# Attention scores on two 64-row tiles of TensorE, both halves of a token tile issued together

## Chip, cores and metric

One core of one Trainium2 chip. The metric is the device time of one execution, in microseconds (us). Lower is better.

## What is computed

Two batches of 1024 tokens of width 256 go through cross-attention to 64 context rows (16 heads of width 16) and then through a mixture of 8 experts, of which each token takes 2. Cut to what matters here:

```
q = layernorm(x) @ w_q.T + b_q;  k = ctx @ w_k.T + b_k;  v = ctx @ w_v.T + b_v      # heads of 16
scores = einsum('bhqd,bhkd->bhqk', q, k) / sqrt(16) + log(key_abundance)
x = x + softmax(scores) @ v @ w_o.T + b_o
x = x + experts(layernorm(x))     # softmax gate, top 2 of 8, silu(x w1) * (x w3) @ w2
```

Everything is float32. The kernel splits the operands of the larger products into two float16 parts (high and low) and adds three products: high by high, high by low, low by high.

## The kernel before

The work has three stages. A preparation (to about 45 us) loads and transposes the weights, makes keys and values, and splits them. The attention stage (to about 180 us) takes the 16 tiles of 128 tokens one per step, with tile `tt` of batch `tt % 2`. The expert stage (from about 210 us) takes 39 tiles of 128 routed tokens. All engines run a program written out by hand (`attention_steps`), with one semaphore for each product; each engine works through its own instructions strictly in order.

**The keys for the scores.** A head has only 16 rows of the contraction. To use all 128 rows of TensorE, `spread_keys` (L799 to L805, on VectorE) writes the keys of 8 heads into a block matrix `kb_hi`, `kb_lo` of 128 rows by 8 x 64 = 512 columns: `head_mask` keeps, for each head, its own 16 rows and clears the other 112. There are four such products for each batch (two groups `c` of 8 heads, high and low), at L803.

**The scores.** `scores_half(par, c)` (L1164 to L1172) makes the scores of 8 heads for 128 tokens in one PSUM bank of `sc_ps`: three matmuls of 512 columns with the query tile (L1169 to L1171) and one of 512 columns that adds the bias and the logarithm of the abundance (`beta`, L1172). One call for `c` = 0 stands at the start of a step, the other for `c` = 1 in its middle.

**One step on TensorE**, in order of the program: scores `c` = 0 of tile t (L1169 to L1172); the product of probabilities and values of tile t-2 (L1204, 8 float32 matmuls, 16 passes); the transpose of the normalized tokens of tile t+1 (L1149); the transpose for the second layer norm of tile t-4 (L1220); scores `c` = 1 of tile t; the transpose of the attention output of tile t-2 (L1232), which waits for `o_norm` and for `xt_lo`; the queries of tile t+1 (L1160 to L1162, 12 matmuls of 128 columns); the transposes of the probabilities of tile t-1 (L1247); the gate's logits of tile t-4 (L1260); the output projection of tile t-2 (L1271, L1272).

**What VectorE and ScalarE do in the same step.** VectorE: maximum of the first 8 heads (L898), reciprocal of the softmax sums (L917, waits for L1204), the scaling of the output (L929, gives `o_norm`), the low part of the next tokens (L834, waits for ScalarE's L632 and gives `xt_lo`), maximum of the other 8 heads (L898 again), subtraction (L945), the low part of the queries (L828), logits (L957), residual (L965), statistics (L970, L906). ScalarE: exponential (L659), high part of the tokens (L632, waits for L1149), two layer norms (L624, L677), L684, the high float16 part of one piece of expert weights (L587), L694, L639, and two copies of the transposed probabilities (L701).

**The expert weights** are prepared beside all this: SyncE loads a piece, ScalarE makes its high part (L587) and GpSimd its low part (L488). Steps 4, 5, 14 and 15 take two pieces, the others one. GpSimd also makes the scale of the second layer norm (L506, L510, L513), behind the pieces that were issued before it.

The product with the values takes the heads pairwise: transposed block `j` holds the probabilities of the two heads that lie at columns 128 j of `sc_ps`, and `v_blk` has the values of heads 2 j and 2 j + 1 in block `j`.

Of the kernel before, what the change touches and what calls it, by code (L numbers as in the profile page):

```python
# [5 lines left out]
ALU = mybir.AluOpType  # L6
ACT = mybir.ActivationFunctionType
F32 = mybir.dt.float32
F16 = mybir.dt.float16
# [3 lines left out]
P = 128  # L13
# [4 lines left out]
def xattn_moe(nc, x, ctx_in, abundance, w_in, b_in, w_out, b_out, gate_w, expert_bias, w1, w2, w3, out):  # L18
# [7 lines left out]
    B, N, D = x.shape  # L26
    S2 = ctx_in.shape[1]
    HD = 16
    H = D // HD
    E, _, F = w1.shape  # L30
# [7 lines left out]
    HS = SL // 2  # L38
    TOPK = 2
    J = (TOK * TOPK + E * (P - 1)) // P  # L40
    NOUT = HD + 1
# [8 lines left out]
    with ExitStack() as stack:  # L50
# [33 lines left out]
        take = Region(arena)  # L84
        xs = take(T * D).rearrange("p (t d) -> p t d", t=T)

        kb_hi, kb_lo = (take(2 * B * HS, F16).rearrange("p (c b n) -> p c b n", c=2, b=B) for _ in range(2))

        wq_hi, wq_lo = (take(KD * D, F16).rearrange("p (k n) -> p k n", k=KD) for _ in range(2))
        xT_hi, xT_lo = take(KD * P, F16), take(KD * P, F16)  # L90
        qT_hi, qT_lo = ([take(2 * P, F16) for _ in range(2)] for _ in range(2))
# [96 lines left out]
        bias16 = take(B * H, F16)  # L188
        ones_row = take(P)[0:1]
        head_mask = take(8)  # L190
        zero_rows = take(D)

        FIRST = 4
# [97 lines left out]
        def here(t, lag):  # L291

            return t is None or 0 <= t - lag < T
# [277 lines left out]
        def _(act):  # L571
# [62 lines left out]
            def queries_high(tt, par):  # L634

                act.wait_ge(s["q_ps"], tt + 1)
                if not isinstance(tt, int) or tt >= 2:
                    act.wait_ge(s["s_ps"], 2 * (tt - 1))
                act.activation(qT_hi[par], bk7[:, 0:2 * P], ACT.Copy).then_inc(s["q_hi_s"], 1)  # L639

            act.wait_ge(s["ln1_shift"], 1)
# [104 lines left out]
        def _(dve):  # L746
# [13 lines left out]
            for c in range(2):  # L760
                dve.tensor_scalar(bq_blk[:, c, :], head_mask[:, :], bias_qk[:, c:c + 1], None, ALU.mult)\
                    .then_inc(s["bq_s"], 1)

            dve.wait_ge(s["ctxT_ps"], 1)
            for k in range(KD):
# [33 lines left out]
            def spread_keys(b):  # L799

                for c in range(2):
                    for dst, src in ((kb_hi, kT_hi), (kb_lo, kT_lo)):
                        dve.tensor_tensor(dst[:, c, b, :].rearrange("p (h s) -> p h s", h=8),  # L803
                                          src[:, c, b:b + 1, :].broadcast_to([P, 8, S2]),
                                          head_mask[:, :, None].broadcast_to([P, 8, S2]), ALU.mult).then_inc(s["kb_dve"], 1)  # L805

            spread_keys(0)

# [80 lines left out]
            def step(u, par, t):  # L889
# [3 lines left out]

                def maxima(c):

                    dve.wait_ge(s["s_ps"], 2 * tt + c + 1)
                    hh = slice(c * H // 2, (c + 1) * H // 2)
                    dve.tensor_reduce(top[:, hh], sv[:, hh, :], AX.X, ALU.max).then_inc(s["smax"], 1)  # L898

# [186 lines left out]
        def _(pe):  # L1086
# [49 lines left out]
            pe.wait_ge(s["bq_s"], 2)  # L1136
            for b in range(B):
                for c in range(2):
                    ins = pe.matmul(bk6[:, b * H + c * 8:b * H + (c + 1) * 8], kT[:, c, b].rearrange("p r s -> p (r s)"),
                                    bq_blk[:, c, :], start=True, stop=True)  # L1140
            ins.then_inc(s["bias_ps"], 1)

            def x_transpose(tt, par):
# [18 lines left out]
                        ins = pe.matmul(o, wq_lo[:, k, cc], xT_hi[:, kk], start=False, stop=k == KD - 1)  # L1162
                ins.then_inc(s["q_ps"], 1)

            def scores_half(par, c):

                o = sc_ps[par][:, c * HS:(c + 1) * HS]
                cc = slice(c * P, (c + 1) * P)
                pe.matmul(o, qT_hi[par][:, cc], kb_hi[:, c, par, :], start=True, stop=False)  # L1169
                pe.matmul(o, qT_hi[par][:, cc], kb_lo[:, c, par, :], start=False, stop=False)  # L1170
                pe.matmul(o, qT_lo[par][:, cc], kb_hi[:, c, par, :], start=False, stop=False)  # L1171
                return pe.matmul(o, ones16[:, :], beta[:, par, c * HS:(c + 1) * HS], start=False, stop=True)  # L1172

            pe.wait_ge(s["bias_parts"], 1)
            x_transpose(0, 0)
# [4 lines left out]
            def step(u, par, t):  # L1180
                tt = 2 * u + par
                if here(t, 0):
                    pe.wait_ge(s["q_lo_s"], tt + 1)
                    if t is None or t >= 2:
                        pe.wait_ge(s["ssub"], tt - 1)
                    elif t == 0:
                        pe.wait_ge(s["kb_dve"], 4)
                        pe.wait_ge(s["beta_s"], 1)
                    elif t == 1:
                        pe.wait_ge(s["kb_dve"], 8)  # L1190
                        pe.wait_ge(s["beta_s"], 2)
                    scores_half(par, 0).then_inc(s["s_ps"], 1)
                if here(t, 2):

                    bt = tt - 2
                    pe.wait_ge(s["pt_sb"], 2 * (bt + 1))
                    if t is None or bt >= 1:
                        pe.wait_ge(s["o_norm"], bt)
                    else:
                        pe.wait_ge(s["v_sb"], 4 * B)  # L1200
                    if here(t, 0):
                        pe.wait_ge(s["q_lo_s"], tt + 1)
                    for j in range(8):
                        ins = pe.matmul(bk7[:, j * 2 * NOUT:(j + 1) * 2 * NOUT], probT[par][:, j * P:(j + 1) * P],  # L1204
                                        v_blk[:, par, j, :], start=True, stop=True)
                    ins.then_inc(s["o_ps"], 1)
                if here(t, -1):
                    if t is None or t >= 3:
# [4 lines left out]
                if here(t, 4):  # L1213
# [5 lines left out]
                    for k in range(KD):  # L1219
                        ins = pe.transpose(pt_ps2[:, k * P:(k + 1) * P], xn2[par][:, k * P:(k + 1) * P], idt)  # L1220
                    ins.then_inc(s["x2t_ps"], 1)
                if here(t, 0):
                    scores_half(par, 1).then_inc(s["s_ps"], 1)
                if here(t, 2):
                    bt = tt - 2
                    pe.wait_ge(s["o_norm"], bt + 1)
# [166 lines left out]
```

## Time and profile before

| | |
|---|---|
| median of 3 runs | 497.25 us (494.78 to 498.67) |
| the profiled execution | 492.84 us |
| its span in the profile | 491.1 us |
| TensorE busy | 402.9 us, 82% of the span |
| VectorE, ScalarE, GpSimd busy | 272.4, 194.7, 223.9 us |
| chain of work that ended last | TensorE 72%, VectorE 11% |

The times of rows are those of the profiled execution, counted from the start of its span; the 1.74 us between its span and its time lie around the program. A row of the timeline has the start, the duration and the engine, then line, operation, what is written and read, and in brackets how long the engine sat idle before it and what ended that. A matmul's recorded duration holds its latency; what it costs in a stream is the distance from its start to the start of the next.

### The profile page before, as it was taken

The numbers are of one execution on the slowest core, as the hardware profiler recorded it, in microseconds if no ns is written. First come the engines' busy times: TensorE is split into PE (matmuls) and PEld (weight loads), VectorE is DVE, ScalarE is ACT, GpSimd is POOL, SyncE is SP. The second block draws the span as 40 slices with busy tenths as digits, with TensorE's granted clock in tenths as the row PEclk, the third lists the DMA queues.
The fourth block names the chain that finished last, engine by engine and source line by source line (L and its number), as shares of the span: only waits on it lengthen the run. The fifth ranks groups of instructions, "written<-read, shape, count | busy, mean of one in ns | idle before, by whom it ended". The sixth has DMA issues, their size and how long they took to land.

```text
span 491.1 us, 10557 instructions
## 1 busy us (share of the span) xinstructions
PE 402.9 (82%) x2969; PEld 303.1 (62%) x2970; DVE 272.4 (55%) x635; ACT 194.7 (40%) x351; POOL 223.9 (46%) x277
## 2 busy tenths in 40 slices
PE   4526998999997531159999999999999999999960
PEld 4303877787776421027777777777777777777740
DVE  2697766767664178915555455555555554555530
ACT  2525677577575433013233323333333333333310
POOL 3694455444446457023444444444444444444321
PEclk9667999999998755569999999999999999999985
DMA  8621442324263623011222222222222222222215
GB/s 263 209 91 61 157 140 86 114 102 133 75 194 108 207 68 92 1 33 24 39 39 43 43 43 43 32 43 35 42 43 43 43 41 35 42 35 43 34 21 182
DMA packets 29267, 38.35 MB, mean 78 GB/s; under 512 B 5173, under 2 KB 23874, under 8 KB 29218
## 3 DMA queue, kind: packets, MB, share of 16 engines
q1 hardware_dynamic: 21440, 27.60, 17.7%
q0 software_dynamic: 7488, 10.39, 13.5%
q8 instruction: 9, 0.15, 0.1%
q10 hardware_dynamic: 322, 0.15, 0.1%
q14 instruction: 8, 0.07, 0.0%
HBM read 28.62 MB, written 11.60 MB: 82 GB/s over the span
## 4 chain that ended last, share of the span: by engine, by line
PE 72%; DVE 11%; issue 4%; DMA 4%; POOL 3%; ACT 3%; POOLq 0%; SPq 0%; DVEq 0%; ACTq 0%
PE sc L1337 10%; PE sc L1339 10%; PE sc L1338 10%; PE ptps L1327 6%; PE bank L1360 6%; PE bank L1356 5%; PE bank L1358 4%; PE bank L1204 4%; PE bank L1271 3%; PE ptps L1247 3%; DVE arena L803 2%; PE bank L1309 2%; DMA arena<-in_x 2%; PE bank L1260 1%; DMA stage_w<-in_L_ffn_w 1%
## 5 line engine op out<-in xcount | busy, mean ns | idle before, releaser
L563 POOL DMA_INDIRECT acc<-arena,put_now x39 | 62.5, 1603 | 113.9 <-DVE arena L1075 113.9
L1337 PE MATMUL sc<-w_hi,arena 128*128 x312 | 98.3, 315 | 1.0 <-DVE arena L1053 1.0
L1338 PE MATMUL sc<-w_hi,arena 128*128 x312 | 98.3, 315 | 0.0
L1339 PE MATMUL sc<-w_lo,arena 128*128 x312 | 98.3, 315 | 0.0
L488 POOL TENSOR_TENSOR w_lo<-stage_w,w_hi 128x1408 f16<-128x1408 f32 (+3 forms) x32 | 73.6, 2312 | 43.7 <-ACT w_hi L587 43.7
L1065 DVE SCALAR_TENSOR_TENSOR arena<-sc,slot_score,arena 128x352 f32<-128x352 f32 (+1 forms) x117 | 53.0, 480 | 66.2 <-ACT arena L734 66.2
L734 ACT ACTIVATE arena<-sc,slot_score 128x352 f32<-128x352 f32 x78 | 43.3, 555 | 89.7 <-PE sc L1339 89.7
L1356 PE MATMUL bank<-w_hi,arena 128*128 x234 | 64.4, 275 | 2.2 <-DVE arena L1080 2.2
L1360 PE MATMUL bank<-w_lo,arena 128*128 x234 | 64.8, 277 | 0.0
L741 ACT ACTIVATE arena<-ptps 128x768 f16<-128x768 f32 x39 | 31.7, 812 | 83.4 <-PE ptps L1327 83.4
L1078 DVE TENSOR_TENSOR arena<-ptps,arena 128x640 f16<-128x640 f32 x39 | 32.2, 825 | 44.4 <-ACT arena L741 44.4
L538 POOL DMA_INDIRECT arena<-table,get_now x39 | 39.7, 1017 | 33.2 <-POOL get_now L535 32.1
L1358 PE MATMUL bank<-w_hi,arena 128*128 x195 | 53.7, 276 | 0.0
L1339 PEld LDWEIGHTS sc<-w_lo,arena 128*128 128x128 f16 x312 | 30.7, 99 | 16.4
L1337 PEld LDWEIGHTS sc<-w_hi,arena 128*128 128x128 f16 x312 | 30.7, 99 | 15.8 <-issue 1.4
L1338 PEld LDWEIGHTS sc<-w_hi,arena 128*128 128x128 f16 x312 | 30.8, 99 | 14.8
L535 POOL COPY get_now<-arena 128x1 int32 (+1 forms) x39 | 28.0, 718 | 22.0 <-DVE arena L1029 15.3
L587 ACT ACTIVATE w_hi<-stage_w 128x1408 f16<-128x1408 f32 (+3 forms) x32 | 35.0, 1104 | 7.3 <-DMA stage_w<-in_L_ffn_w 7.3
L1327 PE MATMUL ptps<-ident,arena 128*128 128x128 f32 x234 | 34.1, 282 | 1.2 <-DVE arena L1065 1.2
L1204 PEld LDWEIGHTS bank<-v_blk,w_lo 128*128 128x128 f32 x256 | 30.9, 192 | 2.2
L1204 PE MATMUL bank<-v_blk,w_lo 128*128 128x34 f32 x256 | 29.9, 272 | 0.0
L1360 PEld LDWEIGHTS bank<-w_lo,arena 128*128 128x128 f16 x234 | 22.9, 98 | 10.8 <-issue 8.4
(198 smaller groups left out, 708.4 us busy)
## 6 DMA issues: line engine op xcount, KB each, us to landing
stage_w<-in_L_ffn_w SPq DMA_DIRECT2D x16, 704.0 KB, 4.3
stage_w<-in_L_ffn_w SPq DMA_DIRECT2D x16, 256.0 KB, 2.8
arena<-in_x SPq DMA_DIRECT2D x2, 1024.0 KB, 7.1
stage_w<-in_L_ffn_w SPq DMA_DIRECT2D x32, 64.0 KB, 2.7
acc<-arena SPq DMA_DIRECT2D x16, 128.0 KB, 1.7
table<-xn SPq DMA_DIRECT2D x16, 128.0 KB, 1.8
arena<-table,get_now POOLq DMA_INDIRECT x39, 2.8
acc<-arena,put_now POOLq DMA_INDIRECT x39, 3.8
```

The source lines that it names most:

```text
L488: pool.tensor_tensor(w_lo[:, cols], staged[:, :], w_hi[:, cols], ALU.subtract).then_inc(s["wlo"], 1)
L563: pool.indirect_dma_start(out=acc[:, :], out_offset=bass.IndirectOffsetOnAxis(ap=put_now[q][:, 0:1], axis=0), in_=y_sb[q], in_offset=None, ...
L734: act.activation(sil[par].rearrange("p (c n) -> p c n", c=2)[:, c, :], h1_ps[:, c, :], ACT.Silu, scale=slot_score[par][:, 0:1]).then_inc(s ...
L1065: dve.scalar_tensor_tensor(out=hid[par][:, at:at + b - a], in0=h3_ps[:, c, a - c * FH:b - c * FH], scalar=slot_score[par][:, 0:1], in1=sil ...
L1204: ins = pe.matmul(bk7[:, j * 2 * NOUT:(j + 1) * 2 * NOUT], probT[par][:, j * P:(j + 1) * P], v_blk[:, par, j, :], start=True, stop=True)
L1327: ins = pe.transpose(hT_ps[:, c * P:(c + 1) * P], hid[q][:, c * P:(c + 1) * P], idt)
L1337: pe.matmul(ps[:, c, :], gT_hi[par][:, kk], w_hi[:, cols], start=k == 0, stop=False)
L1338: pe.matmul(ps[:, c, :], gT_lo[par][:, kk], w_hi[:, cols], start=False, stop=False)
L1339: ins = pe.matmul(ps[:, c, :], gT_hi[par][:, kk], w_lo[:, cols], start=False, stop=k == KD - 1)
L1356: pe.matmul(bk7[:, 0:D], hT_hi[q][:, cc], w_hi[:, cols], start=c == 0, stop=False)
L1358: pe.matmul(bk7[:, 0:D], hT_lo[q][:, cc], w_hi[:, cols], start=False, stop=False)
L1360: ins = pe.matmul(bk7[:, 0:D], hT_hi[q][0:rows, cc], w_lo[0:rows, cols], start=False, stop=c == KF - 1)
```

## The change

`spread_keys` no longer clears all but 16 of 128 rows. It keeps a block of 4 heads for each half of 64 rows: `half_mask` (the sum of the two halves of `head_mask`, one small operation on VectorE) has 4 columns, and `kb_hi`, `kb_lo` have 256 columns for each group `c` where they had 512. Rows 0 to 63 of these 256 columns hold heads 0 to 3 of the group, rows 64 to 127 heads 4 to 7.

The scores of a token tile are then made at one place, at the start of the step: first the two `beta` matmuls of 512 columns, which open both PSUM banks, and then 12 matmuls of 64 rows and 256 columns. They come in pairs: one on rows 0 to 63 that adds to the first bank, one on rows 64 to 127 that adds to the second. The scores of the middle of the step are gone, and `s_ps` counts one for a tile where it counted two; both maxima of VectorE wait for that one. The heads lie in another order in `sc_ps`, so the bias is written in that order, and the product with the values takes its blocks by `jv`.

```diff
+        HQ = HS // 2
+        kb_hi, kb_lo = (take(2 * B * HQ, F16).rearrange("p (c b n) -> p c b n", c=2, b=B) for _ in range(2))
...
+            link(dve.tensor_tensor(half_mask[:, :], head_mask[:, 0:4], head_mask[:, 4:8], ALU.add))
...
-                        dve.tensor_tensor(dst[:, c, b, :].rearrange("p (h s) -> p h s", h=8),
-                                          src[:, c, b:b + 1, :].broadcast_to([P, 8, S2]),
-                                          head_mask[:, :, None].broadcast_to([P, 8, S2]), ALU.mult).then_inc(s["kb_dve"], 1)
+                        dve.tensor_tensor(dst[:, c, b, :].rearrange("p (h s) -> p h s", h=4),
+                                          src[:, c, b:b + 1, :].broadcast_to([P, 4, S2]),
+                                          half_mask[:, :, None].broadcast_to([P, 4, S2]), ALU.mult).then_inc(s["kb_dve"], 1)
...
-                    dve.wait_ge(s["s_ps"], 2 * tt + c + 1)
+                    dve.wait_ge(s["s_ps"], tt + 1)
...
-            def scores_half(par, c):
-
-                o = sc_ps[par][:, c * HS:(c + 1) * HS]
-                cc = slice(c * P, (c + 1) * P)
-                pe.matmul(o, qT_hi[par][:, cc], kb_hi[:, c, par, :], start=True, stop=False)
-                pe.matmul(o, qT_hi[par][:, cc], kb_lo[:, c, par, :], start=False, stop=False)
-                pe.matmul(o, qT_lo[par][:, cc], kb_hi[:, c, par, :], start=False, stop=False)
-                return pe.matmul(o, ones16[:, :], beta[:, par, c * HS:(c + 1) * HS], start=False, stop=True)
+            def scores(par):
+
+                for c in range(2):
+                    pe.matmul(sc_ps[par][:, c * HS:(c + 1) * HS], ones16[:, :], beta[:, par, c * HS:(c + 1) * HS],
+                              start=True, stop=False, skip_group_check=True)
+                for c in range(2):
+                    for q, kb, last in ((qT_hi, kb_hi, False), (qT_hi, kb_lo, False), (qT_lo, kb_hi, True)):
+                        for g in range(2):
+                            rows = slice(g * P // 2, (g + 1) * P // 2)
+                            at = g * HS + c * HQ
+                            ins = pe.matmul(sc_ps[par][:, at:at + HQ], q[par][rows, c * P:(c + 1) * P],
+                                            kb[rows, c, par, :], start=False, stop=last, skip_group_check=True)
+                return ins
...
-                    scores_half(par, 0).then_inc(s["s_ps"], 1)
+                    scores(par).then_inc(s["s_ps"], 1)
...
+                        jv = j % 4 // 2 * 4 + j // 4 * 2 + j % 2
+                        ins = pe.matmul(bk7[:, jv * 2 * NOUT:(jv + 1) * 2 * NOUT], probT[par][:, j * P:(j + 1) * P],
+                                        v_blk[:, par, jv, :], start=True, stop=True)
...
-                if here(t, 0):
-                    scores_half(par, 1).then_inc(s["s_ps"], 1)
```

TensorE in step 4, from its start to the transpose of the attention output. Before:

```order
L1169 MATMUL sc<-arena 128x512
L1170 MATMUL sc<-arena 128x512
L1171 MATMUL sc<-arena 128x512
L1172 MATMUL sc<-beta,ones 128x512
L1204 MATMUL bank<-v_blk,w_lo 128x34 x8
L1149 MATMUL bank<-ident,xn 128x128 x2
L1220 MATMUL ptps<-ident,xn 128x128 x2
L1169 MATMUL sc<-arena 128x512
L1170 MATMUL sc<-arena 128x512
L1171 MATMUL sc<-arena 128x512
L1172 MATMUL sc<-beta,ones 128x512
L1232 MATMUL bank<-ident,o_sb 128x128 x2
```

The same stretch in the changed kernel, whose L1179 is the row-tile matmul, L1214 the values' product, L1153, L1230 and L1240 the three transposes:

```order
L1172 MATMUL sc<-beta,ones 128x512 x2
L1179 MATMUL sc<-arena 128x256 x12
L1214 MATMUL bank<-v_blk,w_lo 128x34 x8
L1153 MATMUL bank<-ident,xn 128x128 x2
L1230 MATMUL ptps<-ident,xn 128x128 x2
L1240 MATMUL bank<-ident,o_sb 128x128 x2
```

Four matmuls of 512 columns stood between the transposes L1220 and L1232; nothing stands there now, and 14 matmuls stand ahead of the values' product where there were 4.

VectorE in the preparation, from the keys of batch 0 to the first maximum, before:

```order
L803 TENSOR_TENSOR arena<-w_hi,w_lo 128x512 [waits kT16]
L803 TENSOR_TENSOR arena<-w_hi,w_lo 128x512 x3
L810 TENSOR_TENSOR arena<-sc,arena 128x512 [waits wq_hi_s]
...
L828 TENSOR_TENSOR arena<-bank,arena 128x256 [waits q_hi_s]
L803 TENSOR_TENSOR arena<-w_hi,w_lo 128x512 x4
L786 BN_STATS w_lo<-arena 128x6 x4
L898 TENSOR_REDUCE top<-sc 128x8 [waits s_ps]
```

The same in the changed kernel:

```order
L806 TENSOR_TENSOR arena<-w_hi,w_lo 128x256 [waits kT16]
L806 TENSOR_TENSOR arena<-w_hi,w_lo 128x256 x3
L813 TENSOR_TENSOR arena<-sc,arena 128x512 [waits wq_hi_s]
...
L831 TENSOR_TENSOR arena<-bank,arena 128x256 [waits q_hi_s]
L806 TENSOR_TENSOR arena<-w_hi,w_lo 128x256 x4
L789 BN_STATS w_lo<-arena 128x6 x4
L901 TENSOR_REDUCE top<-sc 128x8 [waits s_ps]
```

The order is unchanged there; eight operations have half the columns.

## Rows read from the trace of the kernel before

**Rows 1.** TensorE in steps 2 to 5 and 6 to 13: length, busy (instructions), granted clock, DMA share, GB/s
```profile
48.10:78.30 30.20, 28.24 (x224) 1.00 0.41 134
78.31:138.95 60.64, 59.08 (x475) 1.00 0.34 109
```

**Rows 2.** TensorE's timeline in step 11
```profile
116.55 0.38 PE L1169 MATMUL sc<-arena 128*128 128x512 f16 x1
...
117.42 1.87 PE L1204 MATMUL bank<-v_blk,w_lo 128*128 128x34 f32 x16
119.12 0.42 PE L1149 MATMUL bank<-ident,xn 128*128 128x128 f32 x2
...
120.24 0.38 PE L1172 MATMUL sc<-beta,ones 128*128 128x512 f16 x1
120.56 0.41 PE L1232 MATMUL bank<-ident,o_sb 128*128 128x128 f32 x2
...
123.80 0.38 PE L1169 MATMUL sc<-arena 128*128 128x512 f16 x1
```

**Rows 3.** ScalarE and VectorE in step 11
```profile
119.57 0.38 ACT L632 ACTIVATE arena<-bank 128x256 f16<-128x256 f32 x1 [2.42 <-PE bank L1149]
...
119.32 0.26 DVE L917 RECIPROCAL o_inv<-bank 128x16 f32<-128x16 f32 x1 [0.20 <-PE bank L1204]
119.61 0.42 DVE L929 TENSOR_TENSOR o_sb<-bank,o_inv 128x256 f32<-128x256 f32 x1
119.99 0.42 DVE L834 TENSOR_TENSOR arena<-bank,arena 128x256 f16<-128x256 f32 x1
```

**Rows 4.** TensorE in step 16, which has no scores
```profile
157.22 1.87 PE L1204 MATMUL bank<-v_blk,w_lo 128*128 128x34 f32 x16
...
159.90 0.44 PE L1232 MATMUL bank<-ident,o_sb 128*128 128x128 f32 x2 [0.56 <-DVE o_sb L929]
```

**Rows 5.** TensorE's timeline in the expert stage, around a matmul on 64 rows
```profile
240.66 0.27 PE L1360 MATMUL bank<-w_lo,arena 128*128 x1
240.77 0.27 PE L1356 MATMUL bank<-w_hi,arena 128*128 x1
240.98 0.28 PE L1360 MATMUL bank<-w_lo,arena 64*128 x1
241.19 0.87 PE L1327 MATMUL ptps<-ident,arena 128*128 128x128 f32 x6
```

**Rows 6.** GpSimd in step 4, and TensorE in steps 5 and 15
```profile
67.69 5.68 POOL L488 TENSOR_TENSOR w_lo<-stage_w,w_hi 128x1408 f16<-128x1408 f32 x2 [2.67 <-ACT w_hi L587]
...
75.86 1.07 PE L1247 MATMUL ptps<-ident,w_hi 128*128 128x128 f32 x8 [1.25 <-ACT xn2T L684]
...
153.24 1.90 PE L1247 MATMUL ptps<-ident,w_hi 128*128 128x128 f32 x8 [2.74 <-ACT xn2T L684]
```

**Rows 7.** VectorE's and GpSimd's timelines, read from two points each, so later counts are smaller
```profile
24.96 8.63 DVE L803 TENSOR_TENSOR arena<-w_hi,w_lo 128x512 f16<-128x512 f16 x3
28.22 5.37 DVE L803 TENSOR_TENSOR arena<-w_hi,w_lo 128x512 f16<-128x512 f16 x2
...
24.45 13.45 POOL L488 TENSOR_TENSOR w_lo<-stage_w,w_hi 128x1408 f16<-128x1408 f32 x5
27.71 10.19 POOL L488 TENSOR_TENSOR w_lo<-stage_w,w_hi 128x768 f16<-128x768 f32 x4
```

**Rows 8.** TensorE and VectorE in step 1, and TensorE's busy time and clock after it
```profile
39.58 0.61 PE L1169 MATMUL sc<-arena 128*128 128x512 f16 x1 [0.94 <-DVE arena L828]
40.84 0.63 PE L1172 MATMUL sc<-beta,ones 128*128 128x512 f16 x1
...
41.58 0.69 DVE L898 TENSOR_REDUCE top<-sc 128x8 f32<-128x512 f32 x1 [2.05 <-PE sc L1172]
...
42.00:44.00 2.00, 1.60 (x4) 0.50 0.01 4
44.00:46.00 2.00, 1.12 (x16) 0.98 0.00 0
```

More of the change, by code:

```diff
@@ L85, in xattn_moe @@
         xs = take(T * D).rearrange("p (t d) -> p t d", t=T)
-        kb_hi, kb_lo = (take(2 * B * HS, F16).rearrange("p (c b n) -> p c b n", c=2, b=B) for _ in range(2))
+        HQ = HS // 2
+        kb_hi, kb_lo = (take(2 * B * HQ, F16).rearrange("p (c b n) -> p c b n", c=2, b=B) for _ in range(2))
         wq_hi, wq_lo = (take(KD * D, F16).rearrange("p (k n) -> p k n", k=KD) for _ in range(2))
@@ L190, in xattn_moe @@
         head_mask = take(8)
+        half_mask = take(4)
         zero_rows = take(D)
@@ L637, in queries_high @@
                 if not isinstance(tt, int) or tt >= 2:
-                    act.wait_ge(s["s_ps"], 2 * (tt - 1))
+                    act.wait_ge(s["s_ps"], tt - 1)
                 act.activation(qT_hi[par], bk7[:, 0:2 * P], ACT.Copy).then_inc(s["q_hi_s"], 1)
@@ L1138, in _ @@
                 for c in range(2):
-                    ins = pe.matmul(bk6[:, b * H + c * 8:b * H + (c + 1) * 8], kT[:, c, b].rearrange("p r s -> p (r s)"),
-                                    bq_blk[:, c, :], start=True, stop=True)
+                    o = bk6[:, b * H:(b + 1) * H].rearrange("p (g c h) -> p c g h", g=2, c=2)[:, c]
+                    ins = pe.matmul(o, kT[:, c, b].rearrange("p r s -> p (r s)"),
+                                    bq_blk[:, c, :].rearrange("p (g h) -> p g h", g=2), start=True, stop=True)
             ins.then_inc(s["bias_ps"], 1)
@@ L1203, in step @@
                     for j in range(8):
-                        ins = pe.matmul(bk7[:, j * 2 * NOUT:(j + 1) * 2 * NOUT], probT[par][:, j * P:(j + 1) * P],
-                                        v_blk[:, par, j, :], start=True, stop=True)
+                        jv = j % 4 // 2 * 4 + j // 4 * 2 + j % 2
+                        ins = pe.matmul(bk7[:, jv * 2 * NOUT:(jv + 1) * 2 * NOUT], probT[par][:, j * P:(j + 1) * P],
+                                        v_blk[:, par, jv, :], start=True, stop=True)
                     ins.then_inc(s["o_ps"], 1)
```

## The prediction

> **What bounds the kernel now.** I read the page first: TensorE is busiest and carries most of the chain that ended last. Then I cut the attention stage by step. In steps 6 to 13 TensorE is busy 59.08 of 60.64 us at full clock, in steps 2 to 5 28.24 of 30.20 us [rows 1]. That looks like a stage that gets shorter by whatever is taken off TensorE. Busy time does not say so, though: an engine that fills a wait with work that could stand elsewhere is just as busy. So the next view is the timeline of one step, and beside it those of VectorE and ScalarE.
>
> In step 11 the values' product starts at 117.42, the token transpose at 119.12, the last matmul of the second half of the scores at 120.24, and the transpose of the attention output (L1232) at 120.56 [rows 2]. A 512-column matmul takes 0.216 us of the stream: (117.42 - 116.55) / 4, or 0.87 for four. So the second half of the scores is through at 120.46, and L1232 starts 0.10 later. What it waits for is on VectorE: the reciprocal starts at 119.32, just behind the values' product, the scaling at 119.61, the low part of the tokens (L834) at 119.99, ending 120.41; 0.15 later TensorE goes on [rows 3]. L834 also needs ScalarE's L632, 119.57 to 119.95. Both ways start at TensorE's values' product or the transpose right behind it, and neither passes through the scores. From the start of the values' product to L1232 it is 3.14 us, and that is the time of this chain, not of TensorE's work. The second half of the scores has lain inside it for nothing.
>
> Step 16 shows the same place without scores and without L834: 157.22 to 159.90, 2.68 us, of which TensorE idles 0.56 waiting for the scaling L929 [rows 4]. With L834 (0.42 us more) behind it, one gets 3.1 again.
>
> **The change, part by part.**
>
> *The middle of the step.* Four matmuls, 0.87 us, go from inside the 3.14 us. TensorE has 1.70 us of values' product and about 0.5 of transposes left there (the second half of the scores, 0.87 long and through at 120.46, began at 119.59, 0.47 behind L1149), so it will stand idle for about 3.14 - 2.17 = 0.97 us before L1232. Gain: nothing. VectorE's second maximum need not wait for scores any more, but nothing in the step waits for it: its results go into the next step.
>
> *The start of the step.* What stands there is outside the chain and pays in full. Before: 0.87 us. After: two bias matmuls, 2 x 0.216 = 0.43; six pairs of 256 columns; and the change from 128 rows to 64 and back. A 256-column matmul takes 0.11 us (240.66 to 240.77). The expert stage has one matmul on 64 rows in each tile: from the matmul ahead of it 0.21 us and from it to the next 0.21 us, where 0.11 is usual [rows 5]. So each change of the row size costs 0.10, two of them 0.20.
>
> Whether the two matmuls of a pair run beside each other no row of this case shows. If they do fully, a pair costs 0.109 and six 0.65; if not at all, twelve cost 1.31. The start of the step becomes 0.43 + 0.20 + 0.65 = 1.28 us, or 1.94; with the changes of size hidden too it could be 1.08. I take 1.28: each of the two has its own half of the rows and a bank of its own, so nothing that they use is shared but the issue. So +0.41 us for a step, with bounds of +0.21 and +1.07.
>
> On this the Trainium skill speaks twice. Its page TensorE: Matmul & The Clock Gate (Part 3, packing small matmuls) has matmuls on different row groups run together, with some 4 ns between their starts; by that a pair would be 0.113, an estimate, and the step dearer by 0.02. Its page TensorEngine Tiling (Array Packing) (Key Properties) says that changing the tiling mode drains TensorE; the trace agrees, with the 0.10 of each change in rows 5. By the first page alone the change reads as a gain of 0.64 us a step on TensorE, 1.73 to 1.09; it is the chain of rows 3 that speaks against it.
>
> *In how many steps.* Scores are in steps 0 to 15. Steps 2, 3, 4 and 6 to 13 have the pattern above: 11 steps. In step 5, GpSimd works off two pieces of weights, 67.69 to 73.37, before it makes the scale of a layer norm, and TensorE waits 1.25 us for the result at 75.86; that wait swallows the 0.41. In step 15 the like wait is 2.74 us, at 153.24 [rows 6], on a load that was issued behind the residual at the end of step 13, so steps 14 and 15 are hidden as well. 11 x 0.41 = +4.5 us (bounds: 2.3 and 11.8).
>
> *The preparation.* The eight operations of `spread_keys` halve. The first four lie beside GpSimd's and ScalarE's way to the first tokens. The other four are exposed: TensorE's queries of tile 1 come behind them. There the operations take 3.26 us and not their own time: GpSimd's pieces start at 24.45 and 27.71, VectorE's operations end at 24.96 and 28.22, each 0.51 behind the start of the next piece [rows 7]. Read as: each of VectorE's waits for the whole of GpSimd's, then runs in 0.51, and GpSimd waits for it in turn. Halved, only the 0.51 shrinks, to some 0.25: 4 x 0.26 = 1.05 us. Bounds: nothing, and half of what they take in all, 8.63 / 2 = 4.3 for the last three and 0.26 for the first, 4.6.
>
> The Trainium skill's page SBUF — State Buffer (two separate sides) calls the port pair of VectorE and GpSimd an exclusive lock that the loser waits for in full, also when a VectorE operation has two SBUF inputs; the trace agrees, with the 0.51 of rows 7.
>
> Of that 1.05, step 1 gives most back. It runs at half the clock: four score matmuls take 4 x 0.42 = 1.68 us from 39.58 on, and VectorE's maximum starts at 41.58, 0.32 behind their end [rows 8]. Now the maximum needs all scores: at half clock, with every term twice its price at full clock (an estimate), 2 x 0.42 + 6 x 0.21 + 2 x 0.20 = 2.50. From 39.58 - 1.05 = 38.53 that is 41.03, and the maximum starts at 41.35, 0.2 earlier than before. Net -0.2 us (without overlap of the pairs 1.26 more, +1.0). `half_mask` is one operation of 4 columns on VectorE (less than the 0.26 of L917 with 16) ahead of L786, which waits for the load of x, and costs nothing; the reordered bias and blocks change no size.
>
> *The sum.* +4.5 - 0.2 = +4.3 us. Against the profiled execution 492.84 becomes 497.1; that execution was 4.4 below the median of the runs shown. On the median: 497.25 + 4.3 = 501.6.
>
> **The rivals.**
>
> *A, forecast: the chain holds, pairs overlap.* 501.6; its own range is 499.4 (changes of size hidden: +2.3 - 0.2) to 503.5. Chance 0.50.
>
> *B, the pairs do not overlap.* 11 x 1.07 + 1.0 = +12.8: 510.1. For it: no row shows two matmuls at once, and the 0.10 at each change of size looks like weights that are not loaded ahead; if that also happens from tile to tile, TensorE gets near this. Against: same size of tile all through the twelve. Chance 0.22.
>
> *C, the clock rises a step later.* The granted clock is 0.50 until 44 and 0.98 behind it [rows 8], after TensorE's scores from 39.58 on and 1.60 us of work in the 2 us from 42. In the changed kernel the scores of tile 1 end near 41.1 and nothing follows until the queries of tile 2, so the rise may come only in step 2. Its start and values' product (1.28 + 1.71 = 3.0 us) at half clock would cost up to 3.0 more; I take 2.0: 503.6. Chance 0.13.
>
> *D, the other side: TensorE's work is the bound and the wait is not.* If the chain of rows 3 could move ahead, the step would lose 1.73 - 1.28 = 0.45: -5.0 - 0.2 = -5.2, 492.0. It needs L1232 to start less than 2.7 us behind the values' product, in place of 3.14. For it: TensorE busy at 97%, and only 0.1 to 0.2 us of idle before L1232. Against: the rows of VectorE and step 16. It decides once L1232 comes 0.41 earlier. Chance 0.08.
>
> *E, sharing in place of waiting.* If VectorE's slow operations are slow in proportion to their size, the preparation gains 4.6, of which step 1 gives 1.05 - 0.2 = 0.8 back: 4.5 - 3.8 = +0.7, 498.0. Against: the two ends 0.51 behind GpSimd's. Chance 0.07.
>
> **How the numbers follow.** 1% is 5.0 us, about what a measurement of this kernel can tell from no change: faster is below 492.3, slower above 502.2. Faster: most of D, 0.06. Within: two thirds of A, all of E, some of C and D, 0.48. Slower: the rest of A, most of C and all of B, 0.46. The range leaves out D and the tail of B: 497.2 to 510.5. The predicted time is A's.
>
> **What would show it.** Right: in steps 6 to 13 an idle of 0.9 to 1.0 us before L1240 (the old L1232), put down to VectorE's L834 or L929; 3.1 to 3.2 us from the values' product to it; 1.3 us from the first bias matmul to the values' product; starts of a pair a few ns apart and pairs 0.11 apart; TensorE's busy time in the stage down, and the stage longer by some 4 us; GpSimd's pieces at 24 to 35 us shorter by about 0.26 each. Wrong: less than 0.5 us of idle there (D), 0.11 from each row-tile matmul to the next (B), a clock of 0.5 behind 45 us (C), or `spread_keys` of batch 1 taking half its 10 us (E). If the steps with a double piece grow as well, the count of 11 was wrong.

## The result, and the profile after

The changed kernel takes 505.85 us (504.27 to 506.24, 4 runs) where the kernel before takes 496.01 us in the same comparison (4 runs): ratio 1.0228, 95% interval 1.0189 to 1.0267. It is slower by 9.8 us by the medians, by 11 us by the ratio. The ratios of this document leave out executions more than 1.5% above the fastest of the same kernel (among them three of e4's ten, one of e7's ten and six of e12's ten), while medians and ranges are of all. The forecast was slower by 4.3 us. The direction and the place were right; the forecast was less than half of what came.

The page of the changed kernel, its first two parts:

```profile
span 503.7 us, 10743 instructions
...
PE 410.0 (81%) x3065; PEld 312.2 (62%) x3066; DVE 269.8 (54%) x636; ACT 195.4 (39%) x351; POOL 222.2 (44%) x277
...
PEclk9756998989989555558999999999999999999985
```

TensorE is busy 410.0 us, 7 more than before, although the scores of a tile take 1.28 us of it where they took 1.73. The last line says why to look at the clock: in the attention stage, from the fifth digit on, eights stand among the nines. In the timeline of two steps (matmul rows of the queries left out; L1172 bias, L1179 row tiles, L1214 values' product, L1240 transpose of the attention output) one sees what was forecast:

```profile
115.03 0.59 PE L1172 MATMUL sc<-beta,ones 128*128 128x512 f16 x2
115.55 0.83 PE L1179 MATMUL sc<-arena 64*128 64x256 f16 x12
116.31 1.97 PE L1214 MATMUL bank<-v_blk,w_lo 128*128 128x34 f32 x16
118.12 0.41 PE L1153 MATMUL bank<-ident,xn 128*128 128x128 f32 x2
...
119.64 0.41 PE L1240 MATMUL bank<-ident,o_sb 128*128 128x128 f32 x2 [0.89 <-DVE arena L837]
...
123.42 0.59 PE L1172 MATMUL sc<-beta,ones 128*128 128x512 f16 x2
```

The start of the step is 1.28 us (115.03 to 116.31) for 0.87 before, and L1240 waits 0.89 us where [rows 2] left 0.10. From the values' product to it are 3.33 us. The step shown is an even one (10), and those were the longer ones before as well: the values' product of step 10 started at 109.52, and L1232 came 3.22 us later:

```profile
112.74 0.41 PE L1232 MATMUL bank<-ident,o_sb 128*128 128x128 f32 x2
```

In the odd steps it is 3.25 us for the 3.14 of [rows 2]. So the stretch grew by 0.11 us in both kinds of step. That the pairs run beside each other shows in the same timeline read from two later points:

```profile
115.67 0.71 PE L1179 MATMUL sc<-arena 64*128 64x256 f16 x10
...
115.78 0.60 PE L1179 MATMUL sc<-arena 64*128 64x256 f16 x8
```

Ten of the twelve are left at 115.67 and eight at 115.78: two matmuls start at once (to within the hundredth that the rows show), the next two 0.11 later. VectorE's and ScalarE's side of the same step, to be held against [rows 3]:

```profile
118.65 0.38 ACT L634 ACTIVATE arena<-bank 128x256 f16<-128x256 f32 x1 [3.48 <-PE bank L1153]
...
118.32 0.26 DVE L920 RECIPROCAL o_inv<-bank 128x16 f32<-128x16 f32 x1 [0.69 <-PE bank L1214]
118.62 0.42 DVE L932 TENSOR_TENSOR o_sb<-bank,o_inv 128x256 f32<-128x256 f32 x1
119.07 0.42 DVE L837 TENSOR_TENSOR arena<-bank,arena 128x256 f16<-128x256 f32 x1
```

The same chain. L837 starts 2.76 us behind the start of the values' product where L834 started 2.57 behind it in [rows 3]: 0.11 is the longer values' product, and 0.08 is the even step, in which L834 started 2.65 behind it before the change too (112.17 for 109.52). What was not forecast is one step earlier in the same timeline:

```profile
110.17 0.44 PE L1240 MATMUL bank<-ident,o_sb 128*128 128x128 f32 x2 [0.81 <-DVE arena L837]
111.68 1.91 PE L1255 MATMUL ptps<-ident,w_hi 128*128 128x128 f32 x8
```

The eight transposes of the probabilities take 1.91 us of record, 1.04 in the steps around. TensorE ran at the lower of its two clock levels there, a granted clock of 0.50, which is half speed, as its stretches say (length, busy, granted clock, DMA share, GB/s):

```profile
76.50:79.50 3.00, 2.96 (x21) 0.50 0.40 159
89.00:104.00 15.00, 13.13 (x125) 1.00 0.36 111
110.60:113.60 3.00, 3.00 (x23) 0.50 0.38 152
114.00:144.00 30.00, 26.08 (x236) 1.00 0.31 89
144.80:147.80 3.00, 3.00 (x20) 0.50 0.30 118
162.00:180.00 18.00, 16.13 (x68) 0.50 0.39 127
```

In the kernel before the clock is full from 48 to 139 us [rows 1]. The distance from one values' product to the next, step by step in the two timelines, sorts the loss:

| step | before, us | after, us | more |
|---|---|---|---|
| 2, 3, 4 | 6.79, 6.77, 7.83 | 7.31, 7.30, 8.35 | 1.57 |
| 5 (two pieces) | 8.79 | 9.54 | 0.75 |
| 6, 7, 8 | 7.94, 7.25, 7.91 | 8.39, 7.78, 8.38 | 1.45 |
| 9 | 7.25 | 9.39 | 2.14 |
| 10, 11, 12 | 7.90, 7.25, 7.89 | 8.39, 7.78, 8.38 | 1.51 |
| 13 | 7.25 | 9.39 | 2.14 |
| 14, 15 | 7.49, 9.92 | 7.82, 9.97 | 0.38 |
| 16 | 6.64 | 9.24 | 2.60 |

An ordinary step costs 0.45 to 0.53 more, 0.50 in the mean of the nine of them; 11 such make 5.5 us. The half-clock stretches of steps 5, 9 and 13 add 0.75 + 1.6 + 1.6 = 4.0 us, that of step 16 another 2.6. Step 2 begins its values' product 0.9 us later (49.87 for 48.99), and 0.9 us come back after step 17: the first matmul of the experts starts at 227.05 for 214.52, 12.5 later. The expert stage is the same length in both (276.6 us to the end of the span). These 12.5 us are more than the 9.8 of the medians, because the profiled execution of the kernel before (492.84 us) lay 3.2 us below its median and that of the changed kernel 0.4 below.

### The profile page after: what moved, and what is told of

Its sections match the earlier page's. It is cut to its first block, busy times and chain, and to the rows that moved or that the text cites. A ratio compares the mean times of both kernels' runs of the same rounds, so it can differ in the third digit from the quotient of the medians.

```text
span 503.7 us, 10743 instructions
## 1 busy us (share of the span) xinstructions
PE 410.0 (81%) x3065; PEld 312.2 (62%) x3066; DVE 269.8 (54%) x636; ACT 195.4 (39%) x351; POOL 222.2 (44%) x277
## 4 chain that ended last, share of the span: by engine, by line
PE 74%; DVE 12%; DMA 4%; issue 3%; ACT 2%; POOL 1%; POOLq 0%; SPq 0%; DVEq 0%; ACTq 0%
PE sc L1345 9%; PE sc L1347 9%; PE sc L1346 9%; PE ptps L1335 6%; PE bank L1368 6%; PE bank L1214 6%; PE bank L1364 5%; PE bank L1366 4%; PE bank L1279 3%; PE ptps L1255 3%; PE sc L1179 2%; DMA arena<-in_x 2%; DVE arena L806 2%; PE bank L1317 2%; PE bank L1268 2%
## 5 line engine op out<-in xcount | busy, mean ns | idle before, releaser
L490 POOL TENSOR_TENSOR w_lo<-stage_w,w_hi 128x1408 f16<-128x1408 f32 (+3 forms) x32 | 72.4, 2276 | 52.4 <-ACT w_hi L589 52.4
L1214 PEld LDWEIGHTS bank<-v_blk,w_lo 128*128 128x128 f32 x256 | 33.1, 209 | 3.5 <-issue 3.5
L1214 PE MATMUL bank<-v_blk,w_lo 128*128 128x34 f32 x256 | 34.6, 294 | 0.0
```

Of the source, the lines that this page charges most:

```text
L490: pool.tensor_tensor(w_lo[:, cols], staged[:, :], w_hi[:, cols], ALU.subtract).then_inc(s["wlo"], 1)
L1214: ins = pe.matmul(bk7[:, jv * 2 * NOUT:(jv + 1) * 2 * NOUT], probT[par][:, j * P:(j + 1) * P], v_blk[:, par, jv, :], start=True, stop=True)
```

## The experiments

All ratios are to the kernel before on the same chip; the changed kernel is 1.0228.

**e1, the idle filled.** Theory 1: the idle that the move opens lets the granted clock fall. Theory 2: the row tiles do, or the wait can't be filled.

```diff
+                if here(t, 0) and here(t, 2):
+                    for _ in range(4):
+                        pe.matmul(pt_ps2[:, 512:1024], ones16[:, :], beta[:, par, 0:512], start=True, stop=True)
```

> The changed kernel with four matmuls of 512 columns added between the transpose L1230 and the transpose L1240 of every step that has both scores and a values' product; they write a PSUM bank that is free there, and their result is never used. Theory 1 (the idle of 0.8 to 1.0 us before L1240 is what lets the granted clock fall): the added 0.87 us lie inside the idle and cost nothing, the clock stays full in steps 2 to 13, and the time falls by the three half-clock stretches of the attention stage, some 6 us, to about 500. The step itself stays at 0.5 us over the step of before. Theory 2 (the clock falls because matmuls on 64 rows count for less, or the wait is not an idle that can be filled): the clock still falls, or the steps grow by 0.87 each; the time stays at 505.8 or goes to 515.

Measured: 1.0115 (1.0073 to 1.0156), 499.0 us. Four useless matmuls in every step that has both scores and a values' product make the kernel 5 to 6 us faster. L1234 is the filler:

```profile
115.76 1.03 PE L1234 MATMUL ptps<-beta,ones 128*128 128x512 f16 x4
116.81 0.41 PE L1243 MATMUL bank<-ident,o_sb 128*128 128x128 f32 x2
```

From the values' product (113.48) to L1243 are again 3.33 us: the filler costs no time. From 60 to 150 us TensorE is busy 87.53 us, at a granted clock of 1.00; the same stretch of the changed kernel is

```profile
60.00:150.00 90.00, 79.50 (x689) 0.94 0.34 108
```

e1's steps are 8.39 and 7.78, those of the changed kernel at full clock, and its steps 5, 9 and 13 take 8.80, 7.78 and 7.78 where the changed kernel takes 9.54, 9.39 and 9.39: 4.0 us less. It is not this one execution alone: the mean granted clock of the whole span was 0.897 to 0.904 in e1's four and 0.877 to 0.886 in the changed kernel's four. Theory 1 holds: about half the loss is the clock and half the step.

Step 16 is another matter. e1 has it at full clock (6.65 us), but e4, e5 and e8 below, whose clock is full from step 4 to 14, have it at 8.83, 9.24 and 8.82, and the kernel before has its own half-clock stretches from 153.3 to 156.7 us and behind 167 us. So the 2.6 us of step 16 in the changed kernel are not shown to come from the idle of the steps before.

**e2, the move without the row tiles.**

```diff
                     scores_half(par, 0).then_inc(s["s_ps"], 1)
+                    scores_half(par, 1).then_inc(s["s_ps"], 1)
...
-                if here(t, 0):
-                    scores_half(par, 1).then_inc(s["s_ps"], 1)
```

> The kernel before with both halves of the scores issued at the start of the step, in full rows (eight matmuls of 512 columns, no row tiles, two banks as before). It separates the move from the row tiles. Theory 1 (the chain from the values' product over VectorE to L1232 sets the step, and the idle lets the clock fall): 0.87 us more at the start of each of 11 steps, +9.5, and the same idle of about 1 us in the middle, with some half-clock stretches of 1.6 to 2.6 us: 509 to 512. Theory 2 (it is the 64-row matmuls that lower the clock): +9.5 alone, 505.5, clock full. Theory 3 (the move is harmless, the row tiles cost): 496.

Measured: 1.0261 (1.0215 to 1.0307), 506.6 us. The start of a step is 1.73 us, L1231 idles 0.89:

```profile
119.17 1.87 PE L1205 MATMUL bank<-v_blk,w_lo 128*128 128x34 f32 x16
...
122.39 0.41 PE L1231 MATMUL bank<-ident,o_sb 128*128 128x128 f32 x2 [0.89 <-DVE arena L834]
```

From 60 to 150 us the mean clock is 0.96. So the move alone costs all that the change costs, the clock falls without a single row tile, and the row tiles give back some 0.3%, which is inside the intervals. The time is 2 to 5 us under the expectation; the profiled execution has two half-clock stretches before step 15 (in steps 4 and 7), where the changed kernel has three.

**e3, the pairs apart.**

```diff
-                for c in range(2):
-                    for q, kb, last in ((qT_hi, kb_hi, False), (qT_hi, kb_lo, False), (qT_lo, kb_hi, True)):
-                        for g in range(2):
+                for g in range(2):
+                    for c in range(2):
+                        for q, kb, last in ((qT_hi, kb_hi, False), (qT_hi, kb_lo, False), (qT_lo, kb_hi, True)):
```

> The changed kernel with the twelve row-tile matmuls in another order: all six of rows 0 to 63, then all six of rows 64 to 127, so that no two neighbours can run beside each other. If the pairs of the changed kernel overlap: 12 x 0.109 in place of 6 x 0.109, 0.65 us more in each step outside the chain, 13 steps, about +8: 513 to 515. If they never overlapped, 505.8 as the changed kernel. The stretch from the first bias matmul to the values' product should go from 1.28 to 1.9 us.

Measured: 1.0313 (1.0263 to 1.0364), 509.9 us for the 513 to 515 expected. The order was changed as meant, but it did not keep the two halves apart. The start of the step is 1.52 us (120.24 to 121.76), not 1.9. Read from three points:

```profile
120.88 0.94 PE L1179 MATMUL sc<-arena 64*128 64x256 f16 x11
...
120.99 0.83 PE L1179 MATMUL sc<-arena 64*128 64x256 f16 x10
...
121.10 0.72 PE L1179 MATMUL sc<-arena 64*128 64x256 f16 x8
```

Two matmuls start alone, then two start between 120.99 and 121.10: from there on the second row group runs beside the first although it was issued behind all six of it. The 0.24 us more in a step explain 2.6 us of the 4.0 to 4.2 over the changed kernel; the rest fits the clock, 0.91 from 60 to 150 us for 0.94, though that is read from the slowest of four executions. Whether matmuls on half the rows hold the clock less than full ones is e6's question.

**e4, all scores in the middle.** If the place is what costs, the row tiles should pay where they fill the wait. The call of the scores goes with its waits from the start of the step to behind L1230's block, and the first maximum goes from the head of VectorE's step to just ahead of the second, behind the low part of the tokens (L837 of the changed kernel).

```diff
-                    scores(par).then_inc(s["s_ps"], 1)
...
                     ins.then_inc(s["x2t_ps"], 1)
+                    scores(par).then_inc(s["s_ps"], 1)
...
-                    maxima(0)
...
+                    maxima(0)
                     maxima(1)
```

> The changed kernel with all scores of a tile issued in the middle of the step, between the transposes L1230 and L1240, where half of them stood before, and both maxima of VectorE behind the low part of the tokens (L837). Theory 1: the start of the step loses its 1.3 us, the idle of 1.0 us is filled, and only 0.3 to 0.4 us of the scores stick out: a step 0.4 us shorter than before, the clock full, 489 to 492. Rival: VectorE's way through both maxima and the subtraction, now in a row behind L837, or the exponential behind it, becomes the wait that ends last: 496 or more.

Measured: 0.9917 (0.9876 to 0.9959), 490.9 us. The number came, the reason did not. From step 5 on the steps are 7.21 and 7.90, as before. In the profiled execution 3.5 us come from the preparation, where VectorE no longer waits for the scores of tile 1 (values' product of step 2 at 45.46), and 1.3 from steps 2 to 4; steps 15 and 16 give 1.2 back. In the chain of waits of this kernel the step hangs on the second layer norm, from the residual (L967) over GpSimd (L508 to L515) and ScalarE's L679 and L686 to the transposes of the probabilities (L1254):

```profile
105.15 0.43 DVE arena L967
...
106.80 0.23 POOL ve L508
...
107.18 0.58 POOL rs L512
...
107.96 0.28 POOL nmr L515
...
109.04 0.37 ACT xn2T L686
...
109.55 1.06 PE ptps L1254 x8
```

TensorE keeps its full clock in this kernel, although it stands idle in it too: 0.32 and 0.43 us in each even step (as at 109.55 and 111.04) and 0.18 in each odd one.

```profile
60.00:150.00 90.00, 81.18 (x749) 1.00 0.41 126
```

**e5, half the filler.** As e1 with `range(2)`.

> As e1_fill4, with two matmuls of 512 columns (0.43 us) in place of four. The idle before the transpose of the attention output goes from about 0.9 to about 0.5 us. If it is the idle that lets the granted clock fall, there are fewer half-clock stretches in steps 5 to 16 than the four of the changed kernel, and the time lies between e1_fill4 (1.0115 of before) and the changed kernel (1.0228). If the clock stays full with half the filler already, it equals e1_fill4.

Measured: 1.0132 (1.0069 to 1.0194), 500.8 us. The idle before the transpose is 0.45 us, and the clock stays at 1.00 from 60 to 150:

```profile
100.71 0.41 PE L1243 MATMUL bank<-ident,o_sb 128*128 128x128 f32 x2 [0.45 <-DVE arena L837]
```

```profile
60.00:150.00 90.00, 83.19 (x747) 1.00 0.37 113
```

In these executions the clock stayed full with an idle of 0.37 to 0.59 us before the transpose in every step, and with e4's 0.75 in all in every second; it fell with 0.80 to 1.02 in every step. How much idle it takes stays open. From 150 to 200 us, where no filler stands any more, e5 was granted less than e1 (e1's row first):

```profile
150.00:200.00 50.00, 24.53 (x186) 0.71 0.45 136
...
150.00:200.00 50.00, 30.94 (x152) 0.57 0.45 138
```

(The difference to e1 in the ratio is inside the intervals.)

**e6, a filler on half the rows.**

```diff
+                    for _ in range(6):
+                        pe.matmul(pt_ps2[:, 512:768], ones16[0:64, :], beta[0:64, par, 0:256], start=True, stop=True)
```

> As e1_fill4, but the filler is six matmuls of 64 rows and 256 columns, all on rows 0 to 63, 0.65 us and two changes of the row size, 0.85 us in all. Theory 1 (only idle time counts): as e1_fill4, clock full, 1.0115 of before. Theory 2 (what counts is how much of the array works, so that a matmul on half the rows keeps the clock up less): half-clock stretches remain, 1.015 to 1.023.

Measured: 1.0163 (1.0087 to 1.024), 501.7 us. The filler takes the idle away as in e1, but the clock falls once all the same (step 7 takes 9.40 us, 7.78 in e1 and e5). The timeline, and behind it the stretch from 60 to 150 us:

```profile
100.90 0.83 PE L1234 MATMUL ptps<-beta,ones 64*128 64x256 f16 x6
101.85 0.41 PE L1243 MATMUL bank<-ident,o_sb 128*128 128x128 f32 x2
```

```profile
60.00:150.00 90.00, 86.84 (x775) 0.98 0.35 110
```

One profiled stretch leans to theory 2: TensorE is recorded as busier than in e5 (86.84 us for 83.19) and still lost its clock. The ratios of e5 and e6 don't tell the two apart, so it stays a hint.

**e7, the bias last.**

```diff
-                    pe.matmul(sc_ps[par][:, c * HS:(c + 1) * HS], ones16[:, :], beta[:, par, c * HS:(c + 1) * HS],
-                              start=True, stop=False, skip_group_check=True)
-                for c in range(2):
-                    for q, kb, last in ((qT_hi, kb_hi, False), (qT_hi, kb_lo, False), (qT_lo, kb_hi, True)):
+                    for q, kb, first in ((qT_hi, kb_hi, True), (qT_hi, kb_lo, False), (qT_lo, kb_hi, False)):
...
-                                            kb[rows, c, par, :], start=False, stop=last, skip_group_check=True)
+                                            kb[rows, c, par, :], start=first, stop=False, skip_group_check=True)
+                for c in range(2):
+                    ins = pe.matmul(sc_ps[par][:, c * HS:(c + 1) * HS], ones16[:, :], beta[:, par, c * HS:(c + 1) * HS],
+                                    start=False, stop=True, skip_group_check=True)
```

> The changed kernel with the two bias matmuls behind the twelve row-tile matmuls. Behind the change from 64 rows to 128 then stands a float16 matmul and not the first float32 one of the values' product. In the changed kernel the values' product takes 1.81 us to the next transpose where it took 1.70. If that 0.11 is the float32 weight load that can't run ahead across the change, it goes away: the step 0.1 us shorter, 1 us in all. If it comes with the row tiles themselves, nothing changes: 1.0228 of before, and 1.81 us.

The banks are now opened by the row-tile matmuls, each bank twice (once for each `c`), and the kernel no longer adds up the same scores; only its time is read. Measured: 1.0133 (1.0085 to 1.018), 10 runs from 498.1 to 506.5 us. The values' product takes its 1.70 us again:

```profile
114.43 0.83 PE L1176 MATMUL sc<-arena 64*128 64x256 f16 x12
115.19 0.61 PE L1179 MATMUL sc<-beta,ones 128*128 128x512 f16 x2
115.63 1.87 PE L1214 MATMUL bank<-v_blk,w_lo 128*128 128x34 f32 x16
117.33 0.42 PE L1153 MATMUL bank<-ident,xn 128*128 128x128 f32 x2
```

That is the 0.11 us by which the chain had grown. The weight loads (PEld) say where it was: the first ones of the values' product, in the changed kernel and then in e7:

```profile
116.31 0.19 PEld L1214 LDWEIGHTS bank<-v_blk,w_lo 128*128 128x128 f32 x1 [0.21 <-issue]
...
115.42 0.41 PEld L1214 LDWEIGHTS bank<-v_blk,w_lo 128*128 128x128 f32 x2
```

In the changed kernel the first load starts with the values' product (116.31); in e7 it starts 0.21 us ahead of it (115.63), beside the last bias matmul. The 1.2 us of 11 steps do not make up the gain in the ratio, which is some 4.7. The ten executions spread over 8 us, which is what five half-clock stretches of 1.6 us more or fewer are worth; the profiled one, among the slowest, has a mean clock of 0.96 from 60 to 150 us, and so some of them.

**e8, full rows in the middle.** e4's move made on the kernel before.

> As e4_middle (all scores in the middle of the step, both maxima behind the low part of the tokens), but with the eight full-row matmuls and the keys of before. It tells what e4_middle has from the row tiles and what from the move. e4_middle gained 3.5 us in the preparation and nothing in the steps of 7.2 and 7.9 us, where the second layer norm's way from the residual over GpSimd to TensorE now ends last. If that is right, full rows cost little in the steps as long as TensorE stays under it: TensorE's work is 0.45 us more in a step, of which 0.2 to 0.3 were idle, so +2; and the preparation gains 1.1 less: 0.992 + 0.006 = 0.998 of before. If the row tiles were worth their 0.45 in every step, 1.002.

Measured: 0.9939 (0.9897 to 0.998), 492.4 us, against e4's 0.9917 and the 0.998 expected. What e4 has it has from the move, and the row tiles are worth about 1 us there (inside the intervals), as long as the layer norm's loop sets the step.

**e9 to e12, that loop taken off.** ScalarE's second layer norm moves from ahead of L686 to behind the copies L703 (the same block, with its waits), in four kernels: e4, e8, the kernel before, the changed kernel.

```diff
-                if here(t, 3):
...
                             .then_inc(s["pt_sb"], 1)
+                if here(t, 3):
```

> e4_middle, with ScalarE's second layer norm (L679, and its wait for GpSimd) moved from ahead of L686 to behind the copies of the transposed probabilities (L703), so that the copy L686, the piece of weights and L696 no longer stand behind that wait. In e4_middle the loop residual, statistics, GpSimd, L679, L686, probability transposes, projection took 7.2 and 7.9 us and set the step. Theory: with it off the way, TensorE's own work sets the step, 1.81 + 0.47 + 1.28 + 0.25 + 0.66 + 0.88 + 0.39 + 1.06 = 6.8 us; 0.75 less in each of some 11 steps: 0.975 of before, 482. Rival: ScalarE itself (5.3 us busy and its place in the chain) or VectorE's subtraction takes over at once, 0.985 to 0.992.

> e9 with the full-row scores and keys of before. If TensorE sets the step in e9, the row tiles are worth what they take off TensorE, 1.73 - 1.28 - 0.1 = 0.35 us a step in some 11 to 13 steps, plus 1.1 us of the preparation: this kernel is 5 us (0.010) slower than e9. If something else sets the step there, it is 1 to 2 us slower, as e8 against e4.

> The kernel before with the same move of ScalarE's second layer norm, scores where they were. It tells what that move gives alone. In every second step of before, TensorE waits about 0.35 us for L694 behind the wide piece of weights; with 0.5 us less ahead of L694 that goes away, and the chain of the values' product stays. Expected: 5 or 6 steps by 0.3, -2 us, 0.996. If the step of before were bound by the loop over GpSimd, 0.985.

> The changed kernel with the same move of ScalarE's second layer norm. The idle before L1240 hangs on the values' product, L837 and L634 and not on the layer norm, so it stays at 0.8 to 0.9 us, and the granted clock still falls at times. Expected: the same gain of 2 us as for before, 1.018 of before. If the move also frees the idle before L1240, 1.005.

| | ratio | interval | median us |
|---|---|---|---|
| e9, middle, row tiles | 0.9521 | 0.9481 to 0.956 | 470.95 |
| e10, middle, full rows | 0.9607 | 0.957 to 0.9644 | 475.13 |
| e11, scores as before | 0.9706 | 0.9654 to 0.9758 | 480.18 |
| e12, scores as in the change | 0.9934 | 0.9886 to 0.9982 | 495.86 |

e9 runs two steps like this, with no wait on TensorE at all (L1202 is the values' product):

```profile
94.42 1.92 PE L1202 MATMUL bank<-v_blk,w_lo 128*128 128x34 f32 x16
...
96.65 0.59 PE L1171 MATMUL sc<-beta,ones 128*128 128x512 f16 x2
97.18 0.83 PE L1178 MATMUL sc<-arena 64*128 64x256 f16 x12
97.94 0.44 PE L1239 MATMUL bank<-ident,o_sb 128*128 128x128 f32 x2
...
101.19 1.94 PE L1202 MATMUL bank<-v_blk,w_lo 128*128 128x34 f32 x16
```

6.77 us a step (6.8 expected), and yet e9 came 11 us under the 482 expected: its steps 5, 15 and 16 take 6.75, 5.85 and 5.28 for e4's 8.80, 8.89 and 8.83, which I had not counted. e10's steps are 7.09. There the row tiles are worth 0.32 us in every step (0.35 expected) and 4 us in all: TensorE sets the step, and what is taken off it counts. e11 was mis-sized: 15 us and not 2. Its steps are 7.2 and 7.4 for 7.25 and 7.90, and the long ones shrink most: step 5 takes 7.2 for 8.79, step 15 5.3 for 9.92, step 16 5.3 for 6.64. I had counted only ScalarE's 0.5 us ahead of L694 and not that the layer norm's wait for GpSimd (2.74 us in step 15, [rows 6]) stood ahead of everything else on ScalarE. In the kernel before ScalarE itself idles there:

```profile
152.22 0.60 ACT L677 ACTIVATE xn<-arena,nmr,rs 128x256 f32<-128x256 f32 x1 [3.46 <-POOL nmr L513]
```

e12 shows the price of the change again: with the same ScalarE order, the scores at the start of the step cost 2.3% against e11 and 4.3% against e9 (0.9934 / 0.9706 and / 0.9521). By the medians of all executions it is 3.3% and 5.3%; e12's ten spread from 488.4 to 497.1 us, so its own ratio against the kernel before (1.002 by the medians) tells no gain. Against the changed kernel it gained 9 to 10 us by the medians, more than the 2 us I gave it, and 1.018 was wrong for the same reason as e11's.

## Why the prediction was wrong in size

- *What bounds the step.* Right. The chain from the values' product over VectorE's L920, L932, L837 to the transpose held: 3.14 forecast for an odd step, 3.25 measured (3.33 in the even ones, for 3.22 before). e2 shows it without row tiles, e1 by filling the idle at no cost. Rival D (the chain could move ahead) is out.
- *The start of the step.* Right: 1.28 us forecast and measured, with 0.11 for a pair. Rival B (no overlap) is out. That the pairs overlap fully was a choice between two bounds that no row could make, and it came out.
- *The middle of the step: "Gain: nothing."* The failed step. The idle was there (0.81 to 1.02 us, 0.97 forecast), but it was priced at nothing on the ground that TensorE waits anyway. With such an idle in every step the clock fell: half speed in steps 5, 9 and 13, 4.0 us by the table, and e1 gives these 4.0 back. With the 4.3 forecast and the 1.2 of the next point that makes 9.5 us, beside the 9.8 between the medians; that it comes so near is in part chance, since the table is of one execution of each. (The profiled pair has 12.5, of which 2.6 are step 16, whose cause is not shown.) Rival C had the clock only at its rise after the preparation. The rows gave a warning that I did not read: [rows 1] show full clock in a stage without such an idle, and nothing in them shows that it stays full with one.
- *The change of row size.* 0.20 us was right for the start of the step; 0.11 more lie behind it in the values' product, whose first weights don't run ahead of it (rows in e7). e7, where they do, has its 1.70 us back: 1.2 us over 11 steps. It is the term that took the step from 0.41 to 0.50. In [rows 5] the float32 transposes behind the 64-row matmul take 0.71 to the next line (at 241.90) where six by 0.11 would be 0.66; that part of it could have been seen.
- *Eleven steps.* Nearly right for the wait: steps 14 and 15 cost 0.33 and 0.05. Step 5 cost 0.75 and not nothing, because of the clock: in e1 and e5, at full clock, it takes 8.80 and 8.79 for the 8.79 before.
- *The preparation.* Right in its main term. VectorE's operations now end 0.24 behind the start of GpSimd's next piece, 0.25 forecast:

```profile
25.31 7.83 DVE L806 TENSOR_TENSOR arena<-w_hi,w_lo 128x256 f16<-128x256 f16 x3
...
25.07 12.38 POOL L490 TENSOR_TENSOR w_lo<-stage_w,w_hi 128x1408 f16<-128x1408 f32 x5
```

  The four end 8.07 us behind the first piece's start, 33.14, for 9.14 in [rows 7]: 1.07 us less, 1.05 forecast. Rival E (half of 10 us) is out. GpSimd's piece began 0.6 us later than before (25.07 for 24.45), which no row here puts down to the change, so the scores of tile 1 started 0.45 earlier (39.13 for 39.58) and not 1.05. Step 1 gave back 0.55, and nothing reached step 2, which started its scores at 48.22 for 48.12.
- *Rival C* came as well, in step 2: the clock fell to 0.50 behind 45 us, and scores that take 1.28 us took 1.65. I had put 0.13 on it and 2 us; those scores cost 0.37 more, and no other cost of it shows in the rows.
- *The range.* The measured 505.85 us lies above rival A's own range, whose upper end (503.5) follows from no sum in the prediction. It lies inside the whole range only because B and C had widened that, and B did not come at all, C only in small.

## What to carry to other kernels

An engine that is busy 97% of a stage can still be held by a chain: look at what starts right behind a wait, and whether work lying inside the wait would be missed there. Taking work out of a wait was not free on TensorE here, since with the idle in every step the clock fell in three of them; filling it, best with real work, kept the clock. Put the shortened work where the wait is: the same row tiles are worth 1 us behind another wait (e4 to e8) and 4 us where TensorE sets the step (e9 to e10).

## What the runs showed that was not expected

- Useless matmuls made a kernel faster: 1.0228 to 1.0115 with four of 512 columns in each step.
- The granted clock fell three times with 0.80 to 1.02 us of idle in every step; it stayed full with 0.37 to 0.59 in every step (e5) and with 0.75 in all in every second (e4).
- Row tiles on different halves of the rows overlapped even when they were issued six and six (e3): start of the step 1.52 us, where one behind another would be 1.9.
- A float32 matmul right behind a change of row size was 0.11 us dearer than one with two float16 matmuls between (1.81 to 1.70 us, e7).
- The place of one wait on ScalarE was worth more than the whole change: 15 us (e11).
